# First tile of an attention and feed-forward kernel: half-block transposes, a copy moved to VectorE, and a reordered join to the next tile

## What is computed

```python
qkv = (x @ w_qkv.T).reshape(B, S, 3, HEADS, HEAD_DIM).transpose(2, 0, 3, 1, 4)
q = q * cos + _rotate_half(q) * sin
k = k * cos + _rotate_half(k) * sin
scores = einsum('bhqd,bhkd->bhqk', q, k) * scale
keep = (rel >= 0) & (rel < window)               # window is 64
attn = softmax(where(keep, scores, -inf))
x = _layernorm(x + einsum('bhqk,bhkd->bhqd', attn, v) @ w_out.T)
gate = silu(qmatmul(x, w_gate, s_gate))
x = _layernorm(x + qmatmul(gate * qmatmul(x, w_up, s_up), w_down, s_down))
```

## Time and profile before

| | us |
|---|---|
| median of 3 runs | 1244.45 (1243.87 to 1245.71) |
| the profiled execution | 1243.32 |
| its span, first to last instruction | 1241.2 |
| TensorE busy in the span | 1205.1 |

### The profile page before, as it was taken

One profiled execution on the slowest core, in us unless ns is written; L12 is line 12 of the kernel. 1 busy time (PEld: TensorE's weight loads), 2 busy tenths in 40 slices (PEclk: granted clock), 3 DMA queues, 4 the chain that ended last, 5 costly groups with the idle time before them and its releaser, 6 DMA issues.

```text
span 1241.2 us, 24533 instructions
## 1 busy us (share of the span) xinstructions
PE 1205.1 (97%) x8272; PEld 552.8 (45%) x8272; DVE 847.5 (68%) x2543; ACT 572.7 (46%) x1613; POOL 505.9 (41%) x492
## 2 busy tenths in 40 slices
PE   8778899999999999999999999999999999999997
PEld 3323344444444444444444444444444444444443
DVE  6745689655986569765797558975499655975433
ACT  3653288204880248602684028830388114860230
POOL 0532655225560445514554145532555134551230
PEclk9889999999999999999999999999999999999999
DMA  8578965406553275434654156440655418542000
GB/s 269 95 145 227 185 132 104 98 36 127 112 95 81 69 137 103 76 75 98 125 103 90 43 108 124 97 105 35 120 109 97 90 49 143 100 86 43 26 1 34
DMA packets 345048, 123.75 MB, mean 100 GB/s; under 512 B 310112, under 2 KB 328928, under 8 KB 344928
## 3 DMA queue, kind: packets, MB, share of 16 engines
q1 hardware_dynamic: 336768, 107.27, 43.9%
q10 hardware_dynamic: 5040, 8.59, 1.8%
q0 software_dynamic: 3120, 6.29, 1.7%
HBM read 26.69 MB, written 8.39 MB: 28 GB/s over the span
## 4 chain that ended last, share of the span: by engine, by line
PE 73%; DVE 8%; issue 5%; SPq 5%; ACT 3%; DMA 3%; POOL 2%; POOLq 0%; ACTq 0%; DVEq 0%
PE bank L562 33%; PE bank L704 17%; PE bank L568 12%; PE bank L586 7%; SPq L360 3%; PE bank L671 2%; ACT bank L869 2%; DVE fuse L980 1%; DMA xT_sb<-xT_sb 1%; PE bank L651 1%; ACT fuse L824 1%; DVE bank L1032 1%; SPq L382 1%; POOL fuse L471 1%; DVE ffn_tmp L1045 1%
## 5 line engine op out<-in xcount | busy, mean ns | idle before, releaser
L869 ACT ACTIVATE bank<-bank,neg_max,qk_scale 128x128 f32<-128x128 f32 x512 | 219.7, 430 | 54.6 <-DVE neg_max L1038 54.5
L562 PE MATMUL bank<-x1T,wg 128*128 128x512 f16 (+1 forms) x1032 | 242.6, 378 | 0.0
L562 PE MATMUL bank<-x1T,wu 128*128 128x512 f16 x1024 | 241.9, 379 | 0.0
L568 PE MATMUL bank<-wqkv,xT_sb 128*128 128x512 f32 x512 | 235.2, 609 | 0.0
L824 ACT ACTIVATE fuse<-fuse 128x512 f16<-128x512 f32 x120 | 65.7, 617 | 349.1 <-DVE fuse L988 343.5
L704 PE MATMUL bank<-wd,fuse 128*128 128x512 f16 x1024 | 222.3, 379 | 0.0
L466 POOL TENSOR_TENSOR xT_sb<-probs,xT_sb 128x512 f16<-128x512 f32 x112 | 129.6, 1157 | 158.0 <-ACT xT_sb L824 158.0
L488 POOL TENSOR_TENSOR fuse<-fuse 128x512 f16<-128x512 f32 x116 | 131.7, 1167 | 124.1 <-ACT fuse L824 124.0
L471 POOL TENSOR_TENSOR fuse<-ffn_tmp,fuse 128x512 f16<-128x512 f32 x128 | 148.4, 1159 | 70.6 <-ACT fuse L824 69.9
L704 PEld LDWEIGHTS bank<-wd,fuse 128*128 128x128 f16 x1024 | 100.2, 98 | 123.2 <-issue 4.0
L562 PEld LDWEIGHTS bank<-x1T,wu 128*128 128x128 f16 x1024 | 100.2, 98 | 120.6
(11 more groups left out here) (138 smaller groups left out, 1115.7 us busy)
## 6 DMA issues: line engine op xcount, KB each, us to landing
xT_sb<-xT SPq DMA_DIRECT2D x32, 256.0 KB, 3.8
v_cross<-v_own SPq DMA_DIRECT2D x64, 128.0 KB, 2.6
out<-y ACTq DMA_DIRECT2D x32, 256.0 KB, 2.0
qkT<-x SPq DMA_DIRECT2D x28, 256.0 KB, 3.6
wqkv<-w_qkvT SPq DMA_DIRECT2D x2, 1024.0 KB, 8.4
wg<-w_gate POOLq DMA_DIRECT2D x1, 2048.0 KB, 8.2
wu<-w_up POOLq DMA_DIRECT2D x1, 2048.0 KB, 13.7
wd<-w_down POOLq DMA_DIRECT2D x1, 2048.0 KB, 9.8
```

The costliest lines, as they stand in the source:

```text
L562: last = pe.matmul(dst, lhsT, rhs, start=(i == 0), stop=(i == len(pairs) - 1))
L568: last = pe.matmul(dst, xT_sb[:, j, k, :], wqkv[:, k, cols], start=(k == 0), stop=(k == KC - 1))
L869: last = act.activation(unit, unit, ACT.Exp, bias=neg_max[:, s % 2, h // 3, h % 3:h % 3 + 1], scale=qk_scale[:, 2:3], accum_out=row_sum[:, ...
```

## The change

In tile 0 the query and key blocks are transposed in halves (8 heads) and no longer in groups (4 heads): 4 transfers for a block, each twice as wide. The first halves of block 1 wait on a semaphore of their own. SyncE's stream in tile 0 is written anew: the second half of block 1 comes behind step 0, block 2 behind steps 2 and 3, block 3 behind steps 5 and 6, the loads of the next input behind steps 4 and 7 and the tables behind step 8. `cross_v` of tile 0 goes from SyncE to VectorE (2 copies for a block, each behind `split_v`). The rotary products of block 2 are made before the first maxima, those of block 3 behind step 3 and no longer 4; ScalarE splits block 2 behind the first exponentials and block 3 behind step 5; GpSimd makes the lows of block 2 before its first step, and those of block 3 in two pieces. At the end of tile 0, VectorE makes the rotary products of tile 1's block 0 before `keep_o(6)` and no longer behind it. Between tiles, GpSimd's `split_low(a + 1, 0)` goes to the end of the tile in front, in tile 0 ahead of `keep_x1` and of the last two inverse deviations, and SyncE's `turn_qk(a, 0)` goes ahead of the four `turn_x1`. TensorE's stream is the same but for the semaphores that it waits on.

The core of the diff:

```diff
         qk_low = ev("qk_low", NB)
+        first_qk_low = sem("first_qk_low")
         max_done = ev("max_done", STEPS)
...
             if isinstance(a, int) and a == 0:
-                for g in range(NG):
-                    eng.wait_ge(first_qkT_in[j][g], 32)
+                for half in range(2):
+                    eng.wait_ge(first_qkT_in[j][half], 32)
             else:
                 wait(qkT_in[j], eng, a - 1, 31)
+
+        def wait_qk_low(eng, a, j):
+
+            if isinstance(a, int) and a == 0 and j < 2:
+                eng.wait_ge(first_qk_low, j + 1)
+            else:
+                wait(qk_low, eng, a, j)
...
-            def first_turn_qk(j, g):
-                if g == 0:
-                    wait(qk_low, sp, 0, j)
+            def first_turn_qk(j, half):
+                if half == 0:
+                    wait_qk_low(sp, 0, j)
                     sp.sem_inc(passed, 1)
+                heads = slice(half * HEADS // 2, (half + 1) * HEADS // 2)
                 for z, slot in ((0, j), (1, 2 * NB - 1 - j)):
-                    at = (z * HEADS + g * HG) * P
-                    sp.dma_start_transpose(qkT[:, slot, g * HG:(g + 1) * HG, :], split_flat[j % 2][:, at:at + HG * P])\
-                        .then_inc(first_qkT_in[j][g], 16)
+                    at = (z * HEADS + heads.start) * P
+                    sp.dma_start_transpose(qkT[:, slot, heads, :], split_flat[j % 2][:, at:at + HEADS * P // 2])\
+                        .then_inc(first_qkT_in[j][half], 16)
...
                 a = 0
-                for j in range(2):
-                    for g in range(NG):
-                        first_turn_qk(j, g)
-                cross_v(a, 0)
+                first_turn_qk(0, 0)
+                first_turn_qk(0, 1)
+                first_turn_qk(1, 0)
                 for s in range(STEPS):
                     turn_probs(a, s, False)
-                    if s in (1, 2, 7, 8):
-                        j, g = {1: (2, 0), 2: (2, 2), 7: (3, 0), 8: (3, 2)}[s]
-                        first_turn_qk(j, g)
-                        first_turn_qk(j, g + 1)
-                    if s in (4, 6, 8):
-                        cross_v(a, s // 2 - 1)
-                    if s in (6, 9):
+                    if s == 0:
+                        first_turn_qk(1, 1)
+                    if s in (2, 3):
+                        first_turn_qk(2, s - 2)
+                    if s in (4, 7):
                         for j in range(2):
-                            load_xT(a + 1, 2 * (s // 9) + j, False)
-                    if s == 7:
+                            load_xT(a + 1, 2 * (s // 7) + j, False)
+                    if s in (5, 6):
+                        first_turn_qk(3, s - 5)
+                    if s == 8:
                         load_tables(a + 1)
...
                 a, f = t, t - 1
+                if attn:
+                    turn_qk(a, 0)
                 for j in range(NB):
...
                     for j in range(NB):
-                        turn_qk(a, j)
+                        if j:
+                            turn_qk(a, j)
                         if 1 <= j < NB - 1:
...
-            def split_low(a, j, ffn):
-                for i in range(4):
+            def split_low(a, j, ffn, parts=range(4)):
+                for i in parts:
                     wait(qk_high, pool, a, 4 * j + i)
                     last = pool.tensor_tensor(*low_operands(j, i, ffn), ALU.subtract)
-                done(qk_low, last)
+                if parts[-1] == 3:
+                    done(qk_low, last, 1 if ffn or j > 2 else 3)
...
                 rope_sums(a, 2, ffn)
+                split_low(a, 2, ffn)
                 for s in range(STEPS):
                     split_probs(a, s, ffn)
-                    if s == 0:
-                        split_low(a, 2, ffn)
-                    if s == 3:
+                    if s == 2:
                         rope_sums(a, 3, ffn)
-                    if s == 4:
-                        split_low(a, 3, ffn)
+                    if s in (3, 4):
+                        split_low(a, 3, ffn, range(2 * (s - 3), 2 * (s - 2)))
                 for j in range(2):
...
                     pool.dma_start(dst[:, :, :], src.rearrange("(k p) n -> p k n", p=P)).then_inc(wffn_in, 16)
+                split_low(a + 1, 0, True)
+                for j in range(2):
+                    keep_x1(a, j, ffn)
                 for j in range(2, NB):
                     invert_deviation1(a, j)
-                for j in range(NB):
+                for j in range(2, NB):
                     keep_x1(a, j, ffn)
...
                 if attn:
-                    for j in range(NB):
+                    for j in range(1, NB):
                         split_low(a, j, ffn)
...
                         keep_x1(a, j, ffn)
+                if more:
+                    split_low(a + 1, 0, ffn)
...
                 exponentials(a, 0, ffn)
+                split_high(a, 2, ffn)
                 exponentials(a, 1, ffn)
...
                 keep_probs_high(a, 0, ffn)
-                split_high(a, 2, ffn)
                 for s in range(2, STEPS):
...
                         keep_v(a, s // 2 - 1, ffn)
-                    if s == 6:
+                    if s == 5:
                         split_high(a, 3, ffn)
...
-            def split_low(a, j, ffn):
+            def first_split_low(j):
                 for i in range(4):
-                    wait(qk_high, dve, a, 4 * j + i)
-                    last = dve.tensor_tensor(*low_operands(j, i, ffn), ALU.subtract)
-                done(qk_low, last)
+                    wait(qk_high, dve, 0, 4 * j + i)
+                    last = dve.tensor_tensor(*low_operands(j, i, False), ALU.subtract)
+                last.then_inc(first_qk_low, 1)
...
                                                       op0=ALU.mult, op1=ALU.subtract))
+
+            def cross_v(a, j):
+                wait(v_low, dve, a, j)
+                for part, b in ((slice(0, WINDOW), j), (slice(WINDOW, P), j + 1)):
+                    done(v_cross_in[j], dve.tensor_copy(v_cross[part, b, :, :, :].rearrange("p h z d -> p (h z d)"),
+                                                        v_own[part, j, :, :, :].rearrange("p h z d -> p (h z d)")), 16)
...
                 rope_products(a, 1, ffn, range(2))
-                split_low(a, 0, ffn)
+                first_split_low(0)
                 rope_products(a, 1, ffn, range(2, 4))
                 rope_sums(a, 1, ffn)
+                rope_products(a, 2, ffn)
                 maxima(a, 0, ffn)
...
                 bias(a, 1)
-                rope_products(a, 2, ffn)
-                split_low(a, 1, ffn)
+                first_split_low(1)
                 weights(a, 0, ffn)
...
                 split_v(a, 0, ffn)
+                cross_v(a, 0)
                 for s in range(2, STEPS):
...
                         split_v(a, s // 2 - 1, ffn)
-                    if s == 4:
+                        cross_v(a, s // 2 - 1)
+                    if s == 3:
                         rope_products(a, 3, ffn)
...
                     start_x1(a, j, ffn)
-                keep_o(a, STEPS // 2 - 2)
                 carry_keys(a + 1)
...
                 rope_products(a + 1, 0, True)
+                keep_o(a, STEPS // 2 - 2)
                 for j in range(2):
...
```

More of the change, by code:

```diff
@@ L974, in rope_products @@
                     wait(qk_high, dve, a, 4 * (j - 2) + 3)
[L975 removed]
+                    wait_qk_low(dve, a, j - 2)
                 place = rope_place(j, ffn)
```

5 lines of the change are left out of this document (2 added, 3 removed).

## The result

The changed kernel takes 1224.99 us (median of 4 runs, 1222.81 to 1226.02), the kernel before took 1244.16 beside it (1243.87 to 1245.71): ratio 0.9841, 95% interval 0.9824 to 0.9858, some 19 us less. The profiled execution took 1222.81 us with a span of 1221.0.

The account below looks back on a forecast made before the run. SyncE's transfer queue was taken to bound tile 0. Work 92.6, idle 7.5, a half-clock stretch 2.9 and an allowance of 2.5 make 105.5 us for 127.3, hence 1222.6 us in all; range 1217.5 to 1231.

Parts of the forecast that it names:

- 16 x 1.3 = 20.8 us of SyncE spared: Tile 0, SyncE's queue: 16 halves replace 32 groups at the same cost per transfer, sparing 20.8 us of issue time.
- Rival (b): Tile 0: wide transfers served no faster than two narrow ones, about 2.4 us a half; 1234 us, chance 0.08.
- Rival (c): Steps bound by the ScalarE and VectorE chain, each of 13 waiting 0.5 to 1 us more; 1231, chance 0.04.
- Rival (d): Joins to tiles 2 to 7: block 1's pair lands too late behind four transposes; slower, 1250 us, chance 0.04.
- scores 11: Tile 0: the largest wait left, 2.1 us, with ScalarE taking over there from SyncE.
- weights of step 6: Tile 0: these weights arrive 1.0 us late because block 3's halves stand around them.
- No wait: Tile 0, block 1: lows run from near 33.7 to 38.3, half 0 lands by 42.9, ahead of TensorE's scores 4.
- rival (e): VectorE and GpSimd slow each other; copies at 1.2 us each add 3.4 us, 1226 us, chance 0.12.
- 2.9 us behind scores 2: Tile 0: the same half-clock stretch of TensorE as before expected behind step 2's scores, 2.9 us lost.
- 2.5 of allowance: Tile 0: one more half-clock stretch, 1.7 us lost, plus 0.8 us for late landings.
- 3.3 us become 1.2: Join to tile 1: earlier lows and pair of block 0 cut TensorE's wait from 3.3 to 1.2 us.
- the cover on GpSimd: Join to tile 1: delaying the last two inverse deviations about 6 us costs nothing; without cover, up to 4 us.

Follow-up runs that it names:

- e1_groups: Changed kernel with tile 0's query and key transposes in groups of 4 heads again (32 transfers), in the places of the halves: 1236.05 us.
- e5_halves: Kernel before with only the half-block transposes (16 transfers for 32) in the first tile: 1229.2 us, ratio 0.9879.
- e7_gplate: Changed kernel with GpSimd's lows of block 2 put back behind the split of step 0's weights: 1221.5 us, and 1221.96 when repeated.
- e8_maxima: GpSimd's lows of block 2 put back as before in the changed kernel, plus step 1's maxima and bias earlier on VectorE in later tiles: 1219.77 us.
- e0_after: The changed kernel run once more, unaltered, as the measure for other runs: 1226.0 us, ratio 0.9843 to the kernel before.
- e4_early: Changed kernel with VectorE's lows of block 1 moved ahead of its rotary products of block 2: 1225.06 us, ratio 0.9846.

## Why the prediction was right, and where it was off

**The queue.** "16 x 1.3 = 20.8 us of SyncE spared" held: an issue of a half takes 1.34 us where that of a group took 1.27, and it lands after 3.4. e1_groups and e5_halves show from both sides that the number of transfers is what counted. Rival (b), wide transfers no faster, is refuted by the source view. Rival (c) would have shown as small waits in every step; there are two over 1 us behind step 3, at scores 9 and 11. Rival (d) is refuted by the rows of the join to tile 2.

**The idle time.** 7.5 us were forecast, 10.8 came. Scores 0 (0.75 for 0.7), scores 2 (0.96 for 1.6), scores 11 (1.68 for 2.1) and `keep_o` (0.9) came out in size as walked. The weights of step 6, put at 1.0, were not waited for; the 0.8 us at this place are the weights of step 4, whose transpose (issued at 60.33) landed after 4.8 us for the usual 3.3, which is the 0.8 allowed for late landings under the clock. Scores 9 with 1.2 were not foreseen. At scores 11 the size was right and the engine was not: the walk had ScalarE take over, but VectorE works without a break from 62.14 until the weights of step 8 at 66.53, 1.04 us of it on the copies of block 2, and ScalarE waits 0.97 us for VectorE at 66.45. The step that failed is "Block 1: ... the lows ... start near 33.7 and end near 38.3 ... No wait". They started at 35.64, behind the maxima of steps 0 and 1 and the scale of v, and ended near 41.7. The wait was 3.38 us, and the largest, where scores 11 had been named. The size came from 4.6 us as in the earlier trace rows, which was itself a group with GpSimd at work for part of it. The changed order puts both groups exactly side by side: 5.44 to 6.16 us in the five profiles where they are, 2.48 to 2.50 in the five where GpSimd is idle. That is the mechanism of rival (e), mostly in the lows that it names. The copies that it was priced by met it too: one pair of four took 2.15 us for 0.87, beside GpSimd's lows of block 3, and scores 9 wait behind it. (The price itself, 3.4 us for the copies at 1.2 us each, has no working in the prediction; eight copies 0.72 us dearer are 5.8 us, and how many of them lie on the chain isn't said.) The Trainium skill (GPSIMD Engine Reference, Key points) says that VectorE instructions with two SBUF inputs contend with GpSimd. The trace agrees, and e7_gplate shows the size: the term "No wait" measured 3.38 us, and 3 to 4 us of time hung on it. The prediction weighs the rule; what it mis-sized is the group, at 4.6 us for 6.08, and its start, 1.9 us too early.

**The clock.** 2.9 us behind scores 2 and 2.5 of allowance were forecast. Behind scores 2, where TensorE now resumes at 33.44 after 0.96 us, neither profile of the changed kernel has a stretch; this term of 2.9 us measured nothing there. (e7_gplate's profile has one behind the same wait, 0.95 us there, so it is not excluded either.) TensorE's busy time beyond the 92.6 us of work was 1.1 us in one profile and 5.0 in the other (93.69 and 97.62). Of the 5.4 us forecast 0.8 were for late landings, and they came, as idle time. The other 4.6 stand against a mean of 3.1.

**The sum.** Forecast 105.5 us. The two profiles have 104.5 and 107.7, 106.1 in the mean, since 2.9 us too little idle time (10.8 and 10.1 for 7.5) stand against 2.4 us too much for the clock and late landings (5.4, where the profiles show 1.1 and 5.0 of clock). That the sum came within 0.6 us is in good part luck: the two errors are each at least four times as large and cancel.

**The join and the later tiles.** "3.3 us become 1.2" held at scores 1 (0.97), and the lows, the early pair and the cover on GpSimd worked as said. But TensorE then meets the chain of ScalarE and VectorE at scores 4, with 2.35 us. That wait lies behind the first feed-forward product, so it is not in the 105.5 but in the rest, 1086.2 us for 1084.3 before. The forecast ended its walk one wait too soon. e8_maxima shows that this is the chain: 1.1 us of maxima moved into VectorE's gap took 1.35 us off it. With the 0.6 us of the sum these 1.9 us (1.5 in e0_after) account for the 2.4 us between 1222.6 and the measured 1225.0, as far as two profiles can. In neither of the two did a half-clock window follow this wait; in five other profiles one did, for some 1.4 us more, which the forecast's allowance did not look for in this place. The later joins cost nothing, as said.

Open: why e4_early's transfer took 5.34 us, how much of the waits at scores 9 and 11 the copies on VectorE cost, and what decides in an execution how many half-clock stretches follow the same waits.

## What to carry to other kernels

Where small transfers stand in line on one queue, count issues and not bytes, and make them as wide as their consumer allows while the issue stays as cheap (here up to 1024 values; the transposes of 2048 in the later tiles hold the queue for about 2.4 us each, and nothing more is won per value there). Then look for the engine that bounds next, since the further gain of e7_gplate and e8_maxima lay there. Before two engines are given element-wise work with two SBUF inputs at the same time, check that neither has a waiter: one position of one GpSimd call was worth 3 to 4 us here. When a wait is removed, walk on to the next two waits of the same engine, as its chain has not become any shorter.

## What was not expected of the hardware

- VectorE's four 128x512 subtractions of two SBUF inputs took 2.49 us beside an idle GpSimd and 6.08 beside GpSimd's same work, 2.4 times as long; GpSimd's took 4.50 alone and 5.84 beside them, 1.3 times. Two 64x1024 fp16 copies on VectorE, with one input each, went from 0.87 to 2.34 us beside it (e7_gplate), and to 2.15 in the changed kernel.
- The same kernel, with nearly the same waits, had 3.4 us at half clock in one execution and 13.7 in another, and the same wait of 2.3 us had a half-clock window behind it in five profiles and none in three.
